# A four-layer graph network on one core: the attribute term of a perceptron is multiplied a stage earlier, and its last bias is added by GpSimd

## The chip, the cores and the metric

The kernel is written for one NeuronCore of a Trainium2 chip and is one launch. The metric is the device time of the launch in microseconds (us). The engines are TensorE (PE in the rows; its weight loads are PEld), VectorE (DVE), ScalarE (ACT), GpSimd (POOL) and SyncE (SP), which only issues transfers. All data is float32.

## The reference

12500 nodes with 128 features, 200000 edges sorted by destination. Four layers, each read from a layer norm and ReLU of `x` and added to `x`:

```
h = relu(layernorm(x)); x = x + L0(h)   # attention over edges, one head, batch norm
h = relu(layernorm(x)); x = x + L1(h)   # attention, four heads, term from edge_attr_13
h = relu(layernorm(x)); x = x + L2(h)   # perceptron, below
h = relu(layernorm(x)); x = x + L3(h)   # a table of 8 products by edge type, mean over edges

# L2
agg = segment_sum(edge_attr_128, dst)          # [12500, 128], depends on no layer
model_in = concatenate([h, agg, u[0]])         # 3 x 128
h1 = relu(model_in @ W1 + b1)
h2 = relu(h1 @ W2 + b2)
out = h2 @ W3 + b3
```

`W1` has three blocks of 128 rows: one for `h`, one for the attribute sums `agg`, one for `u` (a constant vector, folded into the first bias).

## The kernel before

Nodes lie as 128 partitions by 98 columns, handled in NK = 14 chunks of JB = 7 columns (896 values for each partition). Where a product fills PSUM banks of 512 values, a chunk is split into HALVES of 4 and 3 columns (512 and 384 values). Edges are handled in NG = 98 groups of 16 gathers.

The stages run one after another, with a barrier of all engines between them: the graph's indices, sweep A over the edges (layer L0; the 128 edge attributes are summed beside it), the nodes of L0, sweep B over the edges (layer L1, in `attention_edges`), the nodes stage `nodes_b_stage` (end of L1, all of L2, the table of L3), the sweep of L3, and the output. The nodes stage of L0 turns the attribute sums by transposes and leaves them in DRAM as `attr_turned` (features on the partitions).

**Sweep B.** GpSimd issues 16 gathers of rows of `table_b` for each group (line 1111). VectorE joins them (lines 1225 to 1290), ScalarE takes the exponentials (line 1169) and issues the stores of `sums_b` (line 1125). TensorE has nothing to do until the end of the sweep, and SyncE nothing but some loads there.

**The nodes stage.** Each engine has its own program, written by hand as a loop over i, in which work of several chunks is interleaved. In round i, among others:

- VectorE: the affine step and residual of chunk i-1 (`residual_2`, lines 1899 to 1903) with its statistics (1674 to 1681); the sum of product three and `x` for chunk i-2 (`add_product`, line 1891) and its statistics; the factors of both norms (1692, 1694); the join of chunk i (`v_join`, lines 1417 to 1433); half of the turned chunk i-1 out of PSUM (1876); `add_own` (1911) and statistics of chunk i; half of the turned chunk i-2 (1876); the factors of norm one of chunk i; the logits of chunk i+1.
- ScalarE: second ReLU of i-2 (line 1815), exponential of i (1391, with a table load), copies of three relation products (1823), roots (1685, with a table load), seven activations of norm two for i-1 (1701), a copy, seven of norm three for i-2, the other halves of the turned chunks (1810), two copies, the root of norm one, first ReLU of i-1 (1815), seven activations of norm one for i.
- TensorE: product three of i-2 (bias by a matmul with a row of ones, line 1982, then 4 and 3 products, line 1985); relation products 2 to 5 of i-3 (line 1968); turn of i-1 (1950); relation 6; turn of i-2; product one of i-1 (line 1956: `w1[:, 0, :]` with the turned `h`, `w1[:, 1, :]` with the turned attribute sums `aT`); relation 0 of i-2; product two of i-1 (1956); relation 1.
- GpSimd: only the gathers `node_sums<-sums_b` (line 1327), seven for each chunk, each chunk after the join of the chunk two before it.
- SyncE: loads of own rows, `h` and `aT` (line 1768), stores of the relation table (1773).

A matmul of float32 is shown as two instructions. Every step waits on semaphores for the steps that it reads, and nothing leaves its place in the queue of its engine.

## Time and profile before

| | us |
|---|---|
| median of three runs | 7913.9 (7896.88 to 7914.8) |
| the profiled execution | 7906.07 |
| its span, first to last instruction | 7894.7 |
| sweep B and the barrier behind it, about | 2930 to 5160 |
| the nodes stage, about | 5160 to 5563 |
| GpSimd busy over the span | 5330.8 (68%) |
| VectorE busy | 3626.2 (46%) |
| TensorE, ScalarE busy | 647.8 (8%), 534.2 (7%) |

A row of a table of stretches gives the stretch, its length, then for PE, PEld, DVE, ACT and POOL the busy time and the number of instructions, then the granted clock of TensorE as a share of 2.4 GHz, the mean busy share of the DMA engines, and GB/s. A row of a timeline gives start, duration, engine, line, operation, output<-input, shapes and count; in square brackets stands how long the engine was idle before it and what ended that. A row of the chain of waits gives start, duration and the piece of work to which the time belongs. A row of groups gives line, engine, operation, names, shapes and count, then busy time and mean ns of one, then idle time before them and what ended it.

### The profile page before, as it was taken

The numbers are of one execution on the slowest core, as the hardware profiler recorded it, in microseconds if no ns is written. First come the engines' busy times: TensorE is split into PE (matmuls) and PEld (weight loads), VectorE is DVE, ScalarE is ACT, GpSimd is POOL, SyncE is SP. The second block draws the span as 40 slices with busy tenths as digits, with TensorE's granted clock in tenths as the row PEclk, the third lists the DMA queues.
The fourth block names the chain that finished last, engine by engine and source line by source line (L and its number), as shares of the span: only waits on it lengthen the run. The fifth ranks groups of instructions, "written<-read, shape, count | busy, mean of one in ns | idle before, by whom it ended". The sixth has DMA issues, their size and how long they took to land. (4 is left out here: it accounts for less than half of the span.)

```text
span 7894.7 us, 20407 instructions
## 1 busy us (share of the span) xinstructions
PE 647.8 (8%) x2458; PEld 431.7 (5%) x2458; DVE 3626.2 (46%) x6297; ACT 534.2 (7%) x1434; POOL 5330.8 (68%) x5327
## 2 busy tenths in 40 slices
PE   1100000000000430000000000069200000000000
PEld 1100000000000430000000000034100000000000
DVE  6656666676667565344433344367222222222223
ACT  1100000000000120000000000058000000000000
POOL 5676666666664567777777777621677777777776
PEclk7555555555555665555555555579555555555555
DMA  5456666665665423333333333345333222222322
GB/s 170 127 176 188 186 194 195 195 198 185 193 196 185 143 94 116 104 104 103 98 104 104 104 104 98 99 157 212 121 97 95 94 95 95 91 94 94 95 95 89
DMA packets 324460, 1042.91 MB, mean 132 GB/s; under 512 B 101449, under 2 KB 117964, under 8 KB 286434
## 3 DMA queue, kind: packets, MB, share of 16 engines
q0 software_dynamic: 175072, 371.37, 18.5%
q1 hardware_dynamic: 92914, 452.26, 16.7%
q10 hardware_dynamic: 56336, 217.99, 7.2%
q14 instruction: 119, 0.97, 0.0%
q8 instruction: 19, 0.31, 0.0%
HBM read 527.27 MB, written 513.96 MB: 132 GB/s over the span
## 5 line engine op out<-in xcount | busy, mean ns | idle before, releaser
L2051 POOL DMA_INDIRECT edge_rows<-table_rel,rel_row x1568 | 1602.6, 1022 | 673.5 <-issue 565.3
L1111 POOL DMA_INDIRECT edge_rows<-table_b,src_i x1568 | 1640.8, 1046 | 526.7 <-issue 525.9
L1111 POOL DMA_INDIRECT edge_rows<-table_a,src_i x1568 | 1480.0, 944 | 702.9 <-issue 479.8
L2134 DVE TENSOR_TENSOR edge_rows<-edge_rows,ps 128x1024 f32<-128x1024 f32 x195 | 238.0, 1221 | 1650.6 <-DMA edge_rows<-table_rel,rel_row 1647.3
L1257 DVE TENSOR_TENSOR z<-edge_rows,dst_logit 128x16 f32<-128x16 f32 (+2 forms) x198 | 40.3, 203 | 1174.0 <-DMA edge_rows<-table_b,src_i 1141.4
L1228 DVE TENSOR_TENSOR edge_rows<-edge_rows,ps 128x1032 f32<-128x1032 f32 (+1 forms) x390 | 484.2, 1241 | 190.1 <-remote 137.3
L1225 DVE TENSOR_TENSOR ps<-edge_rows,ps 128x1032 f32<-128x1032 f32 (+1 forms) x390 | 485.7, 1245 | 53.7 <-DVE edge_rows L1228 45.7
L1290 DVE TENSOR_TENSOR edge_rows<-edge_rows,ps 128x2064 f32<-128x2064 f32 (+2 forms) x198 | 456.5, 2306 | 92.5 <-issue 68.3
L1169 ACT ACTIVATE ps<-weight_decay 128x32 f32<-128x32 f32 (+2 forms) x198 | 47.6, 240 | 4099.4 <-issue 2264.2
L844 PE MATMUL ps<-ident,edge_rows 128*128 128x128 f32 x16 | 3.9, 426 | 3902.6 <-DVE edge_rows L1210 2227.9
L1210 DVE TENSOR_TENSOR edge_rows<-edge_rows,ps 128x1024 f32<-128x1024 f32 x195 | 237.0, 1215 | 91.4 <-remote 81.0
L1202 DVE TENSOR_TENSOR ps<-edge_rows,ps 128x1024 f32<-128x1024 f32 x195 | 239.0, 1226 | 58.2 <-DVE edge_rows L1273 58.2
L2120 DVE TENSOR_TENSOR ps<-edge_rows,ps 128x1024 f32<-128x1024 f32 x195 | 239.5, 1228 | 36.0 <-DMA edge_rows<-table_rel,rel_row 29.3
L1327 POOL DMA_INDIRECT node_sums<-sums_b,sum_row x98 | 95.5, 975 | 235.6 <-DVE out_b L1433 172.7
L844 PEld LDWEIGHTS ps<-ident,edge_rows 128*128 128x128 f32 x16 | 3.1, 224 | 3903.2 <-issue 2228.2
L1968 PE MATMUL ps<-w_rel,own_part 128*128 128x512 f32 x392 | 185.6, 611 | 10.5 <-DVE rel L1883 8.9
L949 PE MATMUL ps<-ident,edge_rows 128*1 128x128 f32 (+1 forms) x16 | 3.7, 413 | 2202.9 <-DVE edge_rows L1228 2202.9
L2081 ACT ACTIVATE ps<-keep 128x16 f32<-128x16 f32 x98 | 19.6, 201 | 2111.7 <-issue 1800.4
L1273 DVE TENSOR_TENSOR edge_rows<-weight_decay,z 128x8 f32<-128x8 f32 (+1 forms) x392 | 72.1, 184 | 187.7 <-remote 121.0
L1529 POOL DMA_INDIRECT dst_logit_b<-node_logit_b,start_row x98 | 99.0, 1011 | 86.5 <-DVE node_logit_b L393 57.8
L1327 POOL DMA_INDIRECT node_sums<-sums_a,sum_row x98 | 95.9, 978 | 79.5 <-issue 31.6
L524 POOL DMA_INDIRECT dst_logit_a<-node_logit_a,start_row x98 | 101.1, 1031 | 70.6 <-ACT node_logit_a L376 39.9
(284 smaller groups left out, 2933.1 us busy)
## 6 DMA issues: line engine op xcount, KB each, us to landing
sums_a<-edge_rows SPq DMA_DIRECT2D x98, 2064.0 KB
sums_b<-edge_rows ACTq DMA_DIRECT2D x98, 1120.0 KB
edge_rows<-in_ea SPq DMA_DIRECT2D x98, 1024.0 KB
sums_rel<-edge_rows ACTq DMA_DIRECT2D x98, 1024.0 KB
table_rel<-rel SPq DMA_DIRECT2D x98, 512.0 KB
edge_rows<-table_a,src_i POOLq DMA_INDIRECT x1568
edge_rows<-table_b,src_i POOLq DMA_INDIRECT x1568
edge_rows<-table_rel,rel_row POOLq DMA_INDIRECT x1568
```

Source lines behind the costliest of these rows:

```text
L524: e.indirect_dma_start(out=A.dst_logit, out_offset=bass.IndirectOffsetOnAxis(ap=start_row[:, j:j + 1], axis=0), in_=node_a[:, j, :], in_of ...
L1111: e.indirect_dma_start(out=rows[:, s, i, 0:L.W], out_offset=None, in_=L.table, in_offset=bass.IndirectOffsetOnAxis(ap=src[:, at:at + 1], a ...
L1202: attr_step.append(then(e.tensor_tensor(old_attr, before(g, t)[:, :, L.W:L.WS], bc(keep_now[:, t, :].unsqueeze(2), [P, GK, D]), ALU.mult)))
L1210: done = e.tensor_tensor(now, now, old_attr, ALU.add)
L1225: done = then(e.tensor_tensor(heads(old), heads(before(g, t)), bc(decay_now.unsqueeze(3), [P, GK, H, C + 1]), ALU.mult))
L1228: done = e.tensor_tensor(now, now, old, ALU.add)
L1290: t_weight = then(e.tensor_tensor(now, now, bc(weights.unsqueeze(3), [P, (end - first) * GK, H, C + 1]), ALU.mult))
L1327: e.indirect_dma_start(out=self.buf[:, k % self.depth, b, :], out_offset=None, in_=self.sums, in_offset=bass.IndirectOffsetOnAxis(ap=sum_r ...
L1968: done = e.matmul(ps[:, 4 + 2 * (j % 2) + h, 0:half * D], own_part[:, j, :], w_rel[:, h * half:(h + 1) * half, :].rearrange("p r d -> p (r ...
L2051: e.indirect_dma_start(out=rows[:, s, i, :], out_offset=None, in_=table_rel, in_offset=bass.IndirectOffsetOnAxis(ap=rel_row[:, at:at + 1], ...
L2120: e.tensor_tensor(old, before, keep_now, ALU.mult).then_inc(step.sem, 1)
L2134: i = e.tensor_tensor(steps(g)[:, t, :, :], steps(g)[:, t, :, :], old, ALU.add)
```

## The change

- In sweep B, SyncE first loads the middle block of `W1`, then for each of the 14 chunks loads `attr_turned` and stores the product to a new DRAM tensor `attr_hidden`. TensorE multiplies each half of a chunk into PSUM bank 3, from the first exponential on, and ScalarE copies each half out, one in each of groups 4 to 31, ahead of its own work for the group.
- In the nodes stage `aT` holds chunks of `attr_hidden`. Product one is only the block for `h`. VectorE adds both (`add_hidden`, two instructions) into `mid1`, between the turned chunk i-2 and the factors of norm one; the first ReLU is one activation of 896 values in place.
- The third bias is added to `x` by GpSimd (`add_bias`, one instruction for a chunk) once norm two has read it. In GpSimd's queue it stands behind the gathers of the chunk two further on. The bias matmuls are gone; `add_product` waits for both.

```diff
+    attr_hidden = dram("attr_hidden", [P, NK, JB * P])
...
+            w_attr = sb("w_attr", [P, D])
+            turned = sb("attr_turned_in", [P, 2, JB * P])
+            hidden = sb("attr_hidden_out", [P, 2, JB * P])
+            w_attr_loaded = sem_of("w_attr_loaded", 16)
+            turned_loaded = [sem_of(f"attr_turned_loaded{i}", 16 * turns(NK, 2, i)) for i in range(2)]
+            attr_product = sem_of("attr_product", 2 * NK)
+            hidden_copied = sem_of("attr_hidden_copied", 2 * NK)
+            hidden_stored = [sem_of(f"attr_hidden_stored{i}", 16 * turns(NK, 2, i)) for i in range(2)]
...
+            def attr_products():
+                e.dma_start(w_attr[:, :], io["c_w1"][P:2 * P, :]).then_inc(w_attr_loaded.sem, 16)
+                for k in range(NK + 1):
+                    if inside(k):
+                        if k >= 2:
+                            e.wait_ge(*attr_product.at(2 * (k - 1)))
+                        e.dma_start(turned[:, k % 2, :], attr_turned[:, k, :]).then_inc(turned_loaded[k % 2].sem, 16)
+                    if inside(k - 1):
+                        e.wait_ge(*hidden_copied.at(2 * k))
+                        e.dma_start(attr_hidden[:, k - 1, :], hidden[:, (k - 1) % 2, :]
+                                    ).then_inc(hidden_stored[(k - 1) % 2].sem, 16)
+                for i in range(2):
+                    e.wait_ge(*hidden_stored[i].at(16 * turns(NK, 2, i)))
+
+            if L.AE:
+                attr_products()
...
+            def copy_hidden(k, h):
+                if k >= 2:
+                    e.wait_ge(*hidden_stored[k % 2].at(16 * (k // 2)))
+                i, n = HALVES[h]
+                e.wait_ge(*attr_product.at(2 * k + h + 1))
+                e.activation(hidden[:, k % 2, i * P:(i + n) * P], ps[:, 3, 0:n * P], ACT.Copy
+                             ).then_inc(hidden_copied.sem, 1)
+
...
+                if L.AE and inside(g // 2 - 2):
+                    copy_hidden(g // 2 - 2, g % 2)
...
         def tensor(e):
+            if L.AE:
+                e.wait_ge(*w_attr_loaded.at(16))
+                e.wait_ge(*exped.at(1))
+                for k in range(NK):
+                    e.wait_ge(*turned_loaded[k % 2].at(16 * (k // 2 + 1)))
+                    for h, (i, n) in enumerate(HALVES):
+                        if k + h:
+                            e.wait_ge(*hidden_copied.at(2 * k + h))
+                        e.matmul(ps[:, 3, 0:n * P], w_attr[:, :], turned[:, k % 2, i * P:(i + n) * P],
+                                 start=True, stop=True).then_inc(attr_product.sem, 1)
...
-        w1 = sb("w1", [P, 3, D])
+        w1 = sb("w1", [P, 2, D])
...
+        bias_3 = sem_of("bias_3", NK)
+        hidden_added = sem_of("attr_hidden_added", NK)
...
             def load_attr(k):
                 if k >= 2:
-                    e.wait_ge(*product_1.at(k - 1))
-                e.dma_start(aT[:, k % 2, :], attr_turned[:, k, :]).then_inc(attr_loaded[k % 2].sem, 16)
+                    e.wait_ge(*hidden_added.at(k - 1))
+                e.dma_start(aT[:, k % 2, :], attr_hidden[:, k, :]).then_inc(attr_loaded[k % 2].sem, 16)
...
         def gpsimd(e):
-            for k in range(NK):
-                nodes.p_fetch(e, k)
+            def add_bias(k):
+                if k == 0:
+                    e.wait_ge(*bars_loaded.at(48))
+                e.wait_ge(*norm2.normed.at(k + 1))
+                e.tensor_tensor(chunk(x, k), chunk(x, k), over_nodes(par[:, 2, :]), ALU.add).then_inc(bias_3.sem, 1)
+
+            for i in range(NK + 2):
+                if inside(i):
+                    nodes.p_fetch(e, i)
+                if inside(i - 2):
+                    add_bias(i - 2)
...
                 if name == "c_w1":
-                    data = data.rearrange("(a k) d -> k a d", k=P)
+                    data = data.rearrange("(a k) d -> k a d", k=P)[:, 0:3:2, :]
...
                 if inside(i - 1):
                     if i == 1:
                         e.wait_ge(*bias_1.at(1))
-                    relu(i - 1, product_1, hidden_1, mid1, 2, b12[:, 2:3])
+                    e.wait_ge(*hidden_added.at(i))
+                    e.activation(mid1[:, :], mid1[:, :], ACT.Relu, bias=b12[:, 2:3]).then_inc(hidden_1.sem, 1)
...
             def add_product(k):
                 e.wait_ge(*product_3.at(k + 1))
+                e.wait_ge(*bias_3.at(k + 1))
                 data = chunk(x, k).rearrange("p j d -> p (j d)")
...
+            def add_hidden(k):
+                e.wait_ge(*product_1.at(k + 1))
+                e.wait_ge(*attr_loaded[k % 2].at(16 * (k // 2 + 1)))
+                for h, (i, n) in enumerate(HALVES):
+                    at = slice(i * P, (i + n) * P)
+                    done = e.tensor_tensor(mid1[:, at], aT[:, k % 2, at], ps[:, 2 + h, 0:n * P], ALU.add)
+                    if h == 0:
+                        then(done)
+                done.then_inc(hidden_added.sem, 1)
...
                 if inside(i - 2):
                     turn(i - 2, h3_transposed, h3_turned_v, h3_chunk(i - 2), 0)
+                if inside(i - 1):
+                    add_hidden(i - 1)
...
-            e.matmul(ps[:, 0, 0:1], w1[:, 2, :], u0[:, :], start=True, stop=True).then_inc(u_product.sem, 1)
+            e.matmul(ps[:, 0, 0:1], w1[:, 1, :], u0[:, :], start=True, stop=True).then_inc(u_product.sem, 1)
             e.wait_ge(*bias_1.at(1))
             for i in range(NK + 3):
                 if inside(i - 2):
                     e.wait_ge(*hidden_2.at(i - 1))
-                    if i == 2:
-                        e.wait_ge(*bars_loaded.at(48))
                     for h, (a, n) in enumerate(HALVES):
-                        e.matmul(ps[:, 2 + h, 0:n * P].rearrange("p (n d) -> p n d", d=D), ones[0:1, :],
-                                 bc(par[0:1, 2, :].unsqueeze(1), [1, n, D]), start=True, stop=False)
                         for m in range(n):
                             done = e.matmul(ps[:, 2 + h, m * P:(m + 1) * P], mid2[:, (a + m) * P:(a + m + 1) * P],
-                                            w3[:, :], start=False, stop=m == n - 1)
+                                            w3[:, :], start=True, stop=True)
                     done.then_inc(product_3.sem, 1)
...
                     k = i - 1
                     for ready in (h2_turned_v, h2_turned_s):
                         e.wait_ge(*ready.at(k + 1))
-                    e.wait_ge(*attr_loaded[k % 2].at(16 * (k // 2 + 1)))
-                    product(2, [(w1[:, 0, :], hT2[:, k % 2, :]), (w1[:, 1, :], aT[:, k % 2, :])]).then_inc(product_1.sem, 1)
+                    product(2, [(w1[:, 0, :], hT2[:, k % 2, :])]).then_inc(product_1.sem, 1)
```

`over_nodes` repeats a row of 128 over the seven columns; `Signal.at(n)` is the value that a wait needs; `sem_of` shares one semaphore between stages by name.

## Rows read from the trace of the kernel before

**Rows 1.** Stretches: sweep A, sweep B, start and steady rounds of the nodes stage.

```profile
520.00:2900.00 2380.00, 162.58 (x843) 142.91 (x843) 1557.78 (x2442) 108.55 (x348) 1511.63 (x1591) 0.52 0.58 180
...
3200.00:5160.00 1960.00, 17.69 (x64) 9.37 (x64) 773.50 (x1139) 42.94 (x179) 1448.38 (x1366) 0.50 0.34 101
...
5160.00:5250.00 90.00, 42.07 (x116) 22.62 (x117) 58.54 (x221) 41.11 (x86) 36.08 (x35) 0.64 0.43 137
...
5365.00:5389.00 24.00, 22.48 (x73) 10.91 (x72) 20.27 (x76) 19.93 (x39) 6.60 (x7) 1.00 0.64 231
```

**Rows 2.** Chain of waits, one steady round of the nodes stage.

```profile
5340.74 1.02 ACT rel L1823
...
5351.25 3.01 PE ps L1956 x8
...
5359.23 1.12 PE ps L1982 x2
...
5361.44 0.84 PE ps L1982 x2
...
5364.89 1.02 ACT rel L1823
```

**Rows 3.** Timeline of the same round, VectorE and ScalarE.

```profile
5343.31 0.20 DVE L1692 RECIPROCAL norm_rs<-norm_std 128x7 f32<-128x7 f32 x1 [0.29 <-ACT norm_std L1685]
...
5346.12 1.09 DVE L1429 TENSOR_TENSOR node_sums<-node_sums,self_ex 128x896 f32<-128x896 f32 x1
...
5353.74 0.19 DVE L1692 RECIPROCAL table_rs<-table_std 128x7 f32<-128x7 f32 x1
...
5354.30 1.16 ACT L1815 ACTIVATE mid<-ps,b 128x512 f32<-128x512 f32 x2 [0.60 <-issue]
...
5355.34 2.79 ACT L1701 ACTIVATE out_b<-out_b,table_nb,table_rs 128x128 f32<-128x128 f32 x7
...
5358.17 1.09 DVE L1899 TENSOR_TENSOR out_b<-out_b,par 128x896 f32<-128x896 f32 x1 [2.71 <-ACT out_b L1701]
```

**Rows 4.** Timeline of the first rounds of the nodes stage.

```profile
5201.56 0.17 DVE L1681 TENSOR_SCALAR table_std<-table_mv 128x7 f32<-128x7 f32 x1
...
5204.32 1.16 ACT L1815 ACTIVATE mid<-ps,b 128x512 f32<-128x512 f32 x2 [2.34 <-issue]
...
5215.56 1.15 DVE L1891 TENSOR_TENSOR x<-x,ps 128x512 f32<-128x512 f32 x2 [1.73 <-PE ps L1985]
...
5231.82 1.16 ACT L1815 ACTIVATE mid<-ps,b 128x512 f32<-128x512 f32 x2 [3.51 <-issue]
```

**Rows 5.** Timeline of the last rounds of the nodes stage.

```profile
5504.80 1.09 DVE L1899 TENSOR_TENSOR out_b<-out_b,par 128x896 f32<-128x896 f32 x1 [4.03 <-ACT out_b L1701]
...
5513.71 0.20 DVE L1692 RECIPROCAL norm_rs<-norm_std 128x7 f32<-128x7 f32 x1
...
5533.47 1.15 DVE L1891 TENSOR_TENSOR x<-x,ps 128x512 f32<-128x512 f32 x2 [11.10 <-PE ps L1985]
```

**Rows 6.** Chain of waits, first rounds and last rounds.

```profile
5226.67 5.11 PE ps L1956 x8
...
5521.65 3.01 PE ps L1956 x8
...
5526.38 1.50 PE ps L1956 x4
```

**Rows 7.** Groups by shape, 5268 to 5488 us: first and second ReLU.

```profile
L1815 ACT ACTIVATE mid<-ps,b 128x512 f32<-128x512 f32 x18 | 12.2, 680 | 5.4 <-issue 4.8 <-PE ps L1956 0.6
...
L1815 ACT ACTIVATE mid<-ps,b 128x384 f32<-128x384 f32 x18 | 10.3, 571 | 0.0
```

**Rows 8.** Groups of GpSimd over the span.

```profile
L1111 POOL DMA_INDIRECT edge_rows<-table_b,src_i x1568 | 1640.8, 1046 | 526.7 <-issue 525.9 <-DMA sums_b<-edge_rows 0.8
...
L1111 POOL DMA_INDIRECT edge_rows<-table_a,src_i x1568 | 1480.0, 944 | 702.9 <-issue 479.8 <-DVE edge_rows L1228 223.1
...
L514 POOL MEMSET zero<- 128x1568 f32 x1 | 1.4, 1395 | 0.0
```

## The prediction, written before the changed kernel was run

> **What bounds the kernel now.** I read the stretches first [rows 1]. In sweep B GpSimd is busy 1448.38 of 1960 us and VectorE 773.50; TensorE (17.69) and ScalarE (42.94) are nearly idle. GpSimd's gaps are its own issue time [rows 8], so the sweep runs at its rate: (1640.8 + 526.7) / 1568 = 1.382 us for a gather. The change adds work there, but none to GpSimd or VectorE. It removes work in the nodes stage, 14 chunks in some 400 us. There, in a steady round, PE is busy 22.48 of 24 us at a granted clock of 1.00, DVE 20.27 and ACT 19.93 [rows 1]: three engines near the limit, so a share says little and the chain of waits decides.
>
> The chain [rows 2] repeats every 24.15 us (5340.74 to 5364.89). It goes ACT (relation copy, table load, roots, norms two and three), PE (turn, product one 3.01, relation, product two, relation, product three, of which the bias is 1.12 + 0.84), relation, ACT. Product one and the bias stand on it, so TensorE's side gives up 1.50 + 1.96 = 3.46 us a round. The question is what is late next, and that is read from the timeline of VectorE and ScalarE [rows 3].
>
> **The edits in sweep B.** TensorE's 28 products, ScalarE's 28 copies (0.680 or 0.571 us by the ReLUs of the same shapes [rows 7]) and 28 transfers of 448 KB go to engines and queues that wait. A copy stands ahead of the exponential of its group in ScalarE's queue, and ahead of the store of the group before; ScalarE has 98% of the sweep free, and a group takes 16 x 1.382 = 22 us. If that cover were gone, it would be 28 x 0.63 = 18 us. SyncE has nothing else to issue before the last group. The transfers share the DMA engines with the gathers: 14 x 2 x 0.46 = 13 MB. Bounds: sweep A moves 180 GB/s at a DMA share of 0.58 against 101 GB/s and 0.34, and takes (1480.0 + 479.8 + 223.1) / 1568 = 1.392 us for a gather against 1.382 [rows 1, 8]. Even if that 0.010 us were all due to the transfers, over the 512 gathers of groups 0 to 31 it makes 5 us. The other end is that each transfer holds the gathers for its own bytes: 0.46 MB at 231 GB/s [rows 1] is 2.0 us, 28 of them 56 us. I take 0; the pair of sweeps is the nearest row.
>
> **The nodes stage, steady.** I follow VectorE once around.
>
> - From the affine step (line 1899) to the factors of norm two (1692): in the round of the drain that VectorE itself sets, 5504.80 to 5513.71 is 8.91 us [rows 5]. In the steady round the same way is 5358.17 to 5343.31 + 24.15 = 5367.46, that is 9.29 [rows 3]: VectorE has only about 0.38 us of slack there.
> - From there to the point where `add_hidden` now stands, just ahead of the factors of norm one: 5343.31 to 5353.74, 10.43 us, without a wait of any length [rows 3].
> - New: two adds of 512 and 384 from PSUM, as line 1891, 1.15 us [rows 4, 5]. Product one is ready: half of it ends at 5351.25 + 1.50 = 5352.75 [rows 2], 1.0 us before.
> - New: ScalarE sees it (0.04), and the ReLU is one of 896. From 680 and 571 ns [rows 7]: 0.85 ns an element, so 680 + 384 x 0.85 = 1.01 us, and norm one starts about 0.94 after it, since the present pair of 1.16 is followed after 1.04 [rows 3].
> - From norm one on ScalarE (5355.34) to the affine step (5358.17): 2.83 us [rows 3].
>
> Sum: 8.91 + 10.43 + 1.15 + 0.04 + 0.94 + 2.83 = 24.30 us. So VectorE and ScalarE together hold the round at 24.30 where TensorE would allow some 20.7; the round gets 0.15 longer, not 3.46 shorter. The first ReLU is the hinge: now it waits for product one at 5354.30, then for VectorE, which comes to the add only at 5353.74, and ends 5355.9 instead of 5355.46. From the first steady affine step to 5504.80 there are 11 rounds: + 1.6 us.
>
> **Start and drain.** In round 1 the first ReLU waits for product one until 5204.32, VectorE is free for the add at 5201.65 [rows 4]: 5201.65 + 1.15 + 0.04 = 5202.84, 1.5 earlier, and norm one 1.6. In round 2 VectorE waits 1.73 us for product three [rows 4]; that goes: 3.3 in all. Then product one on the slow clock takes 5.11 from 5226.67 [rows 6]; with some 2.9 for its half the ReLU starts at 5226.67 - 3.3 + 2.9 + 1.19 = 5227.5 instead of 5231.82 [rows 4], and norm one is 4.4 early. At the end, product one ends 1.50 earlier, the add and wait cost 1.18, the ReLU 1.04 and a hand-over: ReLU done at 5521.65 + 1.50 + 1.18 + 1.08 = 5525.4, product two 1.0 earlier than 5526.38 [rows 6], and product three 1.96 shorter, with VectorE waiting for it [rows 5]: -2.9. Together -7.3 + 1.6 = -5.7 us.
>
> **The bias on GpSimd.** Its waits are harmless: it needs norm two of chunk k (ended 5346.6) and must be done before `add_product` of the next round, which follows product three (from 5359.23 on [rows 2]); GpSimd, queued behind it with the next gathers, waits for the join's end near 5349.3 anyway (line 1429 and two more instructions of its kind [rows 3]); a late start by 2 us of gathers that are used a round later costs nothing. But it runs while VectorE is in the join, the part of its loop in which nearly every instruction reads two operands of SBUF, and VectorE is now on the path. No row shows GpSimd reading SBUF as an operand. Its duration: a memset of 1568 elements took 1.395 us [rows 8], 0.89 ns an element, so 0.80 us for 896 with one stream and 2.4 with three (two read, one written); I take 2.0, nearer to three streams, as there are three. Its effect on VectorE: from 0 to the whole add plus one instruction under way (2.4 + 0.5 = 2.9). If it gets in before line 1431 it holds VectorE some 2.1 us, if it waits for the end of the join it holds `add_own` by some 1.5. I take 1.9 as the likelier case, a judgement. It meets a join in 13 rounds: 13 x 1.9 = + 24.7.
>
> The Trainium skill (SBUF — State Buffer, § Who interferes with whom) says that a VectorE instruction with two SBUF inputs contends with a GpSimd instruction that reads SBUF, and that whoever issues first has the shared ports for its whole instruction. No row of before can show it. By it the hold is sure; without it the sum is -5.7. The GPSIMD Engine Reference (§ 3.1, the same skill) gives 2.6 cycles an element for such an add, by which it would take an estimated 1.9 us.
>
> **Forecast.** -5.7 + 24.7 = + 19 us on the profiled execution of 7906.1, so 7925. The median of before, 7913.9, lies 7.8 higher and its runs span 18 us; I put the forecast between, at 7929.
>
> **The rivals.**
>
> 1. GpSimd and VectorE do not hold each other: -5.7, so 7908. For it: the gathers of GpSimd beside VectorE's joins leave line 1429 at 1.09 us. Against it: those gathers read little. Chance 0.27.
> 2. The add holds VectorE for longer, in 13 rounds over 2.3 us: 13 x 2.9 - 5.7 = + 32, 7946. It is slower by more than 0.3% from 2.3 us a round. Chance 0.14.
> 3. The transfers slow the gathers in sweep B. Half of the upper end, 28 us, on top of the forecast: 7957. Against it sweep A's rate. Chance 0.07.
> 4. TensorE's clock falls in the steady rounds, as PE will be busy 19 of 24 to 26 us. It is granted 1.00 at 22.48 of 24 and 0.64 as the mean of the start, where PE is busy 42.07 of 90 [rows 1]. At 1.2 GHz PE's 19 us would be 38, and a round 14 us longer; if it happens in four of them, + 56 us, 7985. Chance 0.05.
> 5. The round follows TensorE and ScalarE after all, because VectorE runs its loop faster than my walk: ScalarE's 19.93 busy plus its two short waits make 22.8, so 11 x -1.35 - 7.3 = -22, 7892. Against it: the walk's terms are VectorE's own. Chance 0.05.
>
> The forecast has 0.42. A measurement of this kernel can tell some 0.3% (24 us) from no change. Slower: the upper part of the forecast (0.07), rivals 2, 3 and 4 nearly whole (0.23): 0.30. Faster: half of rival 5 and a little of rival 1 with the spread of the runs (0.03): 0.06. Within: 0.64. The range takes in rival 1 with half the spread of the runs and rival 2 with some of it: 7898 to 7955.
>
> **What would show it.** Right: the steady round is about 26.2 us; the first ReLU ends the idle time of ScalarE after VectorE's add, not after a product; VectorE waits for norm one less than 2.71 us, PE waits more; one instruction of the join in each round starts or lasts some 2 us late beside GpSimd's add; the sweep's 98 groups take what they took, within 5 us. No hold: round of 24.3 us and all join instructions at 1.09. Wrong altogether: a steady round below 23.5 us, PE's clock below 1.00 in steady rounds, gathers above 1.40 us each, or VectorE waiting for product one.

## The result and the profile after

The changed kernel takes 7919.45 us (median of 17 runs, 7910.24 to 7938.63); the kernel before, on the same chip, 7909.85 (17 runs, 7891.21 to 7920.99). The ratio is 1.0015 with a 95% interval of 1.0009 to 1.0022: slower by 0.15%, 9.6 us. The forecast was 7929, within 7898 to 7955. The profiled execution took 7917.39 with a span of 7906.2, so 11.3 us more than that of before (7906.1, 7894.7).

The page of the changed kernel, groups of GpSimd, beside [rows 8]:

```profile
L1120 POOL DMA_INDIRECT edge_rows<-table_b,src_i x1568 | 1636.6, 1044 | 530.9 <-issue 530.9
...
L1120 POOL DMA_INDIRECT edge_rows<-table_a,src_i x1568 | 1480.9, 944 | 708.1 <-issue 478.1
...
L1845 POOL TENSOR_TENSOR x<-x,par 128x896 f32<-128x896 f32 x14 | 33.8, 2417 | 195.4 <-ACT hn L1746 195.4
```

A gather of sweep B still takes (1636.6 + 530.9) / 1568 = 1.382 us, to the third digit what it took before. The new add takes 2417 ns in the mean.

The stretches answering to [rows 1] (sweep B, the start of the nodes stage, a part of a steady round, and two whole steady rounds; columns: the stretch, its length, busy us of PE, PEld, DVE, ACT and POOL with instructions, granted clock, DMA share, GB/s):

```profile
3200.00:5158.00 1958.00, 48.86 (x100) 18.16 (x100) 773.14 (x1138) 51.08 (x198) 1443.86 (x1366) 0.50 0.36 105
5158.00:5248.00 90.00, 37.15 (x110) 19.99 (x110) 67.47 (x227) 43.99 (x91) 42.33 (x39) 0.63 0.44 142
5367.00:5391.00 24.00, 18.05 (x60) 8.43 (x58) 21.11 (x65) 19.14 (x38) 9.08 (x8) 1.00 0.60 213
...
5341.00:5367.00 26.00, 20.48 (x66) 9.67 (x65) 23.03 (x79) 20.19 (x39) 9.09 (x8) 1.00 0.62 222
5393.00:5419.00 26.00, 20.54 (x64) 9.95 (x63) 23.04 (x77) 20.28 (x38) 9.08 (x8) 0.93 0.56 203
```

In sweep B TensorE has 31 us more work and ScalarE 8, and GpSimd's and VectorE's sums stay. In the nodes stage VectorE is now the busiest engine, 23.03 of 26 us. The chain of waits over one round says the same (start, length, what it was in), beside [rows 2], where VectorE hardly stood:

```profile
5335.24 1.10 DVE out_b L1967
...
5344.15 0.21 DVE norm_rs L1737
...
5347.02 1.03 DVE node_sums L1474
5348.05 2.91 DVE own_rows L1476
5350.98 1.09 DVE out_b L1478
...
5356.48 1.15 DVE mid L1959 x2
5357.65 1.04 ACT mid L1920
5358.69 1.95 ACT out_b L1746 x6
...
5361.42 1.10 DVE out_b L1967
```

The affine step (line 1899 before, 1967 now) comes every 26.18 us, and up to the ReLU at 5357.65 the chain never leaves VectorE. One of three neighbours in the join, all of the same shape, takes 2.91 us where the others take 1.03 and 1.09. The timeline shows who is beside it:

```profile
5346.95 1.09 DVE L1474 TENSOR_TENSOR node_sums<-node_sums,self_ex 128x896 f32<-128x896 f32 x1
5347.53 2.46 POOL L1845 TENSOR_TENSOR x<-x,par 128x896 f32<-128x896 f32 x1 [12.91 <-ACT hn L1746]
5347.96 2.98 DVE L1476 TENSOR_TENSOR own_rows<-own_rows,self_ex 128x896 f32<-128x896 f32 x1
```

GpSimd's add runs 5347.53 to 5349.99. VectorE's L1476 is issued at 5347.96 and ends at 5350.94, 0.95 after the add: it did nearly all of its work of 1.08 only once the add was over, and lost 1.90.

Where the time went, on the two profiled executions:

| stretch | before | after | difference |
|---|---|---|---|
| up to the first load of the nodes stage | 5160.27 | 5158.03 | -2.2 |
| from there to the third affine step | 75.42 | 72.47 | -2.95 |
| 11 rounds to the last affine step | 269.11 | 288.20 | +19.1 |
| drain, to the first load of the next stage | 57.84 | 55.44 | -2.4 |
| the rest | 2332.07 | 2332.01 | -0.1 |

The 11 rounds would have cost 11 x (26.18 - 24.15) = 22.3; the 3.2 that are missing were two long rounds of before, in which a relation product ran at the lower clock (chain of the kernel before; the granted clock is 1.00 over the first of these pieces and 0.57 over the second):

```profile
5307.48 1.72 PE ps L1968 x4
...
5313.43 3.12 PE ps L1968 x4
```

In 5393 to 5419 of the changed kernel the granted clock is 0.93 as well, and the round still takes 26.18: TensorE has slack now. Of the -2.2 ahead of the stage, 1.8 lie behind the last gather of sweep B, where both kernels do the same: from its end to the first load of the stage it is 58.8 us before and 57.0 after. It is scatter: two kernels below that share the changed sweep, with the memset and with the short add, take 57.0 and 58.8 there too.

### The profile page after: what moved, and what is told of

It is laid out like the page before. It is cut to its first block and busy times, and to the rows that moved or that the text cites. A ratio compares the mean times of both kernels' runs of the same rounds, so it can differ in the third digit from the quotient of the medians.

```text
span 7906.2 us, 20448 instructions
## 1 busy us (share of the span) xinstructions
PE 657.9 (8%) x2402; PEld 425.0 (5%) x2402; DVE 3663.6 (46%) x6325; ACT 548.0 (7%) x1448; POOL 5355.3 (68%) x5341
## 5 line engine op out<-in xcount | busy, mean ns | idle before, releaser
L1120 POOL DMA_INDIRECT edge_rows<-table_b,src_i x1568 | 1636.6, 1044 | 530.9 <-issue 530.9
L1845 POOL TENSOR_TENSOR x<-x,par 128x896 f32<-128x896 f32 x14 | 33.8, 2417 | 195.4 <-ACT hn L1746 195.4
```

Of the source, the lines that this page charges most:

```text
L1120: e.indirect_dma_start(out=rows[:, s, i, 0:L.W], out_offset=None, in_=L.table, in_offset=bass.IndirectOffsetOnAxis(ap=src[:, at:at + 1], a ...
```

## The experiments

All were timed or profiled beside the kernel before on the same chip. Chips differ: on two, no gather was slowed (944 ns in both sweeps) and the kernel before takes 7100 us instead of 7910. The steady rounds of the nodes stage are the same on all of them, so I compare these ("round" is the usual distance of two affine steps), and beside them the stage's length from its first load to that of the next stage. The length scatters more: for the nodes stage of before it is 402.4 us in the trace of [rows 1 to 6] and 399.4 in that of the sweep-only kernel below.

### The bias left out

```diff
             for i in range(NK + 2):
                 if inside(i):
                     nodes.p_fetch(e, i)
-                if inside(i - 2):
-                    add_bias(i - 2)
...
-                e.wait_ge(*bias_3.at(k + 1))
```

> The third bias is left out of the computation: GpSimd's adds and VectorE's waits for them are gone, all else is as after the change. Theory: in each of 13 rounds GpSimd's add holds one instruction of VectorE's join (2.98 us instead of 1.09) through the SBUF access they share, and VectorE's own loop sets the round. Then the steady round is 24.3 us (26.18 with the add), the second instruction of the join lasts 1.09, and the time is some 24 us below the changed kernel and 5 to 12 us below the kernel before. Rival one: the round grew because of VectorE's added instructions and the longer way to the first ReLU, and the held instruction only fills a wait: the round stays above 25.5 us. Rival two: TensorE sets the round once the add is away: below 23.5 us and more than 20 us below the kernel before.

Measured: 7094.11 us against 7100.51, ratio 0.999 (0.9981 to 0.9999). Stage 393.4 us, round 24.28 us (timeline, VectorE):

```profile
4751.57 1.09 DVE L1964 TENSOR_TENSOR out_b<-out_b,par 128x896 f32<-128x896 f32 x1 [2.22 <-ACT out_b L1746]
...
4764.28 1.08 DVE L1476 TENSOR_TENSOR own_rows<-own_rows,self_ex 128x896 f32<-128x896 f32 x1
4765.40 1.09 DVE L1478 TENSOR_TENSOR out_b<-own_rows,node_sums 128x896 f32<-128x896 f32 x1
...
4775.85 1.09 DVE L1964 TENSOR_TENSOR out_b<-out_b,par 128x896 f32<-128x896 f32 x1 [2.21 <-ACT out_b L1746]
```

L1476 is back at 1.08. The walk of the prediction gave 24.30 for a round without a hold; here it is, 24.28. From there to 26.18 are 1.90 us, and by 1.90 one instruction of each round is longer in the changed kernel.

### The bias part alone, and the attribute part alone

The first has the third bias on GpSimd as the changed kernel, and layer one as before. The second has the sweep's products and VectorE's `add_hidden`, and the bias on TensorE:

```diff
                     for h, (a, n) in enumerate(HALVES):
+                        e.matmul(ps[:, 2 + h, 0:n * P].rearrange("p (n d) -> p n d", d=D), ones[0:1, :],
+                                 bc(par[0:1, 2, :].unsqueeze(1), [1, n, D]), start=True, stop=False)
                         for m in range(n):
                             done = e.matmul(ps[:, 2 + h, m * P:(m + 1) * P], mid2[:, (a + m) * P:(a + m + 1) * P],
-                                            w3[:, :], start=True, stop=True)
+                                            w3[:, :], start=False, stop=m == n - 1)
```

> The kernel before with only the bias edit: the bias matmuls go, GpSimd adds the bias after norm two, product one keeps both blocks. Theory: the hold is there without the attribute edit, the second or third instruction of the join lasts 2.9 us in 13 rounds. VectorE has no add of the hidden part, so its loop is 1.15 us shorter: way to norm one 10.43 + 1.83 + 0.40, then 2.83 and 8.91, a round of 24.4 us; against the kernel before (24.16 in its undisturbed rounds, 24.46 on average) no difference in the steady rounds and 2 to 4 us less at start and drain. Rival (the hold needs the added instructions of the attribute edit, or does not matter): join instructions of 1.09 and a round of 23.8.

> The changed kernel with only the attribute edit: the bias is a matmul again, GpSimd adds nothing. Theory: VectorE sets the round at 24.3 us although TensorE has its 1.96 us of bias back, no join instruction above 1.1 us; the time is some 2 us above the kernel without any bias (start and drain), 3 to 10 us below the kernel before. Rival (TensorE is still on the path): the round is longer than without the bias by up to 1.96 us.

Measured: bias alone 7100.51 us, ratio 1.0 (0.9991 to 1.001), round 24.73, stage 399.6. Attribute part alone 7109.45 us, ratio 1.0014 (1.0005 to 1.0023), stage 409.0, with six rounds of 24.67 and five of 26.3.

Bias alone, timeline of a round:

```profile
4762.74 1.09 DVE L1910 TENSOR_TENSOR out_b<-out_b,par 128x896 f32<-128x896 f32 x1 [1.76 <-ACT out_b L1701]
...
4775.03 2.46 POOL L1799 TENSOR_TENSOR x<-x,par 128x896 f32<-128x896 f32 x1 [11.47 <-ACT hn L1701]
4775.46 2.98 DVE L1431 TENSOR_TENSOR own_rows<-own_rows,self_ex 128x896 f32<-128x896 f32 x1
...
4787.47 1.09 DVE L1910 TENSOR_TENSOR out_b<-out_b,par 128x896 f32<-128x896 f32 x1 [1.76 <-ACT out_b L1701]
```

The hold is there in full, 2.98 against 1.08, yet the round is only 0.57 above the 24.16 of before. It is also 0.3 above the 24.4 that I expected, and the 2 to 4 us of gain did not come: the time is that of the kernel before.

Attribute part alone, timeline of a long round and a piece of a usual one:

```profile
4732.79 1.09 DVE L1964 TENSOR_TENSOR out_b<-out_b,par 128x896 f32<-128x896 f32 x1 [2.21 <-ACT out_b L1746]
...
4737.95 2.77 PE L2035 MATMUL ps<-w_rel,own_part 128*128 128x512 f32 x3
4741.20 1.02 ACT L1877 ACTIVATE rel<-ps 128x1024 f32<-128x1024 f32 x1 [4.01 <-PE ps L2035]
4743.78 0.20 DVE L1737 RECIPROCAL norm_rs<-norm_std 128x7 f32<-128x7 f32 x1 [1.99 <-ACT norm_std L1730]
...
4759.15 1.09 DVE L1964 TENSOR_TENSOR out_b<-out_b,par 128x896 f32<-128x896 f32 x1 [2.21 <-ACT out_b L1746]
...
4765.87 1.02 ACT L1877 ACTIVATE rel<-ps 128x1024 f32<-128x1024 f32 x1 [2.33 <-PE ps L2035]
...
4783.82 1.09 DVE L1964 TENSOR_TENSOR out_b<-out_b,par 128x896 f32<-128x896 f32 x1 [2.21 <-ACT out_b L1746]
```

I had expected this one below the kernel before, and it came 9 us above it. Between affine step and the factors of norm two, ScalarE waits 2.33 us for the relation product that stands behind product three and its bias, and the factors come 9.30 us after the affine step instead of 8.91. In the long rounds, where the granted clock of 4734 to 4758 is 0.93 and three of its matmuls take 2.77 together, it waits 4.01. From the kernel without any bias this one differs by the bias matmuls alone, so they keep TensorE on the path: 24.67 against 24.28, and rounds that the lower clock can lengthen. So my theory for this kernel was wrong and its rival right. The attribute part needs TensorE relieved of the bias; the bias part, on VectorE, is dearer beside the attribute part (next experiment).

### The add moved behind VectorE's join

```diff
             def add_bias(k):
                 ...
                 e.wait_ge(*norm2.normed.at(k + 1))
+                if inside(k + 1):
+                    e.wait_ge(*added_h1.at(k + 2))
                 e.tensor_tensor(chunk(x, k), chunk(x, k), over_nodes(par[:, 2, :]), ALU.add).then_inc(bias_3.sem, 1)
```

Once on the changed kernel, and once on the kernel with the bias part alone (here twice, in two sessions).

> The changed kernel, all of the computation, with one more wait in GpSimd's bias add: it waits until VectorE has done the add of h1 for the next chunk. There VectorE has some 4 us in which no instruction reads two operands from SBUF (statistics, a copy from PSUM, the add from PSUM). Theory of the shared read access: GpSimd's add of 2.4 us runs beside them without holding anything, the join's instructions last 1.09, the round is 24.3 us, the time 20 us or more below the changed kernel and 5 to 12 us below the kernel before. GpSimd's gathers start 3.7 us later in a round, which costs nothing. Rival (any VectorE instruction beside GpSimd's add is held): the statistics or the copies take the 1.9 us instead and the round stays at 26 us.

> The kernel before with the third bias on GpSimd, its add held back until VectorE's own-row add of the next chunk is issued; the attribute part stays on TensorE. Theory (the hold is all that the bias part costs, 1.9 us in a round of 24.73 us in which TensorE also had less to do): no join instruction over 1.2 us, steady round 23.8 us, between 22.8 and 24.1, and 4 to 10 us under the kernel before. Rival (the round is set by something that the hold only hides behind): round stays at 24.7 us.

> The kernel with the third bias on GpSimd behind VectorE's own-row add and nothing else of the change, once more and in another session, because where the gathers of sweep B are slowed (1.38 us each and not 1.25) the rest of the kernel is 800 us longer. Theory (the gain lies in the nodes stage alone): that stage within 1 us of 389.3 and 10 to 16 us under the kernel before, whatever the gathers do. Rival (the gain came with the session): within 5 us of the kernel before.

The changed kernel with the add moved: 7093.19 us against 7100.51, ratio 0.999 (0.9981 to 0.9999); round 24.28, stage 393.2, as without any bias.

```profile
4766.52 1.09 DVE L1478 TENSOR_TENSOR out_b<-own_rows,node_sums 128x896 f32<-128x896 f32 x1
...
4768.13 1.08 DVE L1981 TENSOR_TENSOR out_b<-out_b,h 128x896 f32<-128x896 f32 x1
...
4769.36 2.09 POOL L1847 TENSOR_TENSOR x<-x,par 128x896 f32<-128x896 f32 x1 [13.52 <-DVE out_b L1981]
4770.73 0.58 DVE L1723 BATCH_NORM_AGGREGATE table_mv<-stats 128x2 f32<-128x6 f32 x7
```

The add now lies beside VectorE's statistics, which read one operand; nothing is held (every join instruction 1.08 or 1.09), and the add itself is shorter, 2.09 instead of 2.46. So the add costs nothing by its own length: all of its price was the place. 7.3 us under the kernel before is within the 5 to 12 expected.

The bias part alone with the add moved: 7087.09 us against 7099.18, ratio 0.9984 (0.9975 to 0.9993), the fastest kernel here; round 23.77 (theory 23.8), stage 389.3. The gain of 12.1 us is larger than the 4 to 10 expected.

```profile
4804.36 1.09 DVE L1912 TENSOR_TENSOR out_b<-out_b,par 128x896 f32<-128x896 f32 x1 [2.73 <-ACT out_b L1701]
...
4821.03 2.09 POOL L1801 TENSOR_TENSOR x<-x,par 128x896 f32<-128x896 f32 x1 [12.28 <-DVE out_b L1924]
...
4824.25 1.16 ACT L1827 ACTIVATE mid<-ps,b 128x512 f32<-128x512 f32 x2 [0.59 <-PE ps L1969]
...
4828.12 1.09 DVE L1912 TENSOR_TENSOR out_b<-out_b,par 128x896 f32<-128x896 f32 x1 [2.74 <-ACT out_b L1701]
```

Here the first ReLU waits 0.59 us for TensorE's product one, so VectorE has slack just behind the join; that is why the same hold cost this kernel only 24.73 - 23.77 = 0.96. The rest of its 1.90 came out of VectorE's wait for norm one ahead of the affine step, 2.74 here and 1.76 with the hold. In the changed kernel `add_hidden` puts VectorE itself in front of that ReLU, and the hold costs all of its 1.90. In the other session: 7899.55 against 7908.21, ratio 0.999 (0.998 to 0.9999), stage 386.8 against the 402.4 in the trace of [rows 1 to 6]. The stage was 2.5 shorter than I expected and the time 8.7 lower, between the rival's 5 and my 10 to 16; medians of runs that span 34 us don't settle that, the stage does: it is 12.6 below even the 399.4 of the sweep-only kernel, so the gain is there.

### The changed kernel again, the sweep's part alone, and a copy given to ScalarE

The sweep-only kernel has all of the diff ahead of the nodes stage, and the nodes stage of before. The third is the changed kernel with the add moved and

```diff
-        by_vector = (3,)
+        by_vector = ()
...
                     relation(i - 3, 2)
+                    relation(i - 3, 3)
                 if inside(i - 1):
                     norm2.s_root
```

> The changed kernel itself, unaltered, for a comparison with its variants on one chip. Theory (the bias add holds one VectorE instruction in each round): steady round 26.2 us, one join instruction of 2.9 to 3.0 us in each round against 1.09 for its neighbours, time 8 to 16 us above the kernel before. Rival (the loss was a matter of the chip on which it was first timed): within 3 us of the kernel before.

> Only the second sweep's part of the change: the products with the attribute rows of the first layer's weights, their copies and stores; the nodes stage is that of the kernel before, and what is stored is not read. Theory (the sweep is held by the gathers): sweep B within 1 us of before per 98 groups, time within 5 us of the kernel before. Rival (its loads, products and copies slow the sweep): 10 to 50 us slower.

> The changed kernel with the bias add held back until VectorE's own-row add of the next chunk is issued, and the fourth relation copy of each chunk (1.22 us on VectorE) done by ScalarE behind the third. Theory (the round is now the chain of VectorE and ScalarE, and VectorE's copy is on it): root of norm two 0.3 us later, VectorE's 1.22 us gone, so a round of 23.4 us against 24.28 with the add moved alone, about 10 us less over the stage; TensorE no longer waits 2.4 us for that copy. Rival (ScalarE becomes the bound): round 24.6 us or more, slower than with the add moved alone.

The changed kernel: 7116.18 us against 7099.18, ratio 1.0025 (1.0015 to 1.0035); round 26.18, 13 held instructions of 2.86 to 2.98, stage 416.1. The loss is no matter of one chip; at +17.0 it is nearer to the forecast's +19 here, and 1 us above the 8 to 16 that I expected of this run.

The sweep's part: 7099.49 against 7099.18, ratio 1.0001 (0.9992 to 1.001), gathers at 1.25 us, as in the kernel with the bias part alone on the same chip, whose sweep is that of before. It is free within the interval of 0.1%.

The copy on ScalarE: 7095.39 us, ratio 0.9995 (0.9986 to 1.0004), rounds of 24.3 to 25.0, 24.6 in the mean, not 23.4.

```profile
4787.49 1.02 ACT L1881 ACTIVATE rel<-ps 128x1024 f32<-128x1024 f32 x1 [0.69 <-PE ps L2039]
4788.53 1.28 ACT L1730 ACT_TABLE_LOAD   x1
...
4790.06 0.20 DVE L1737 RECIPROCAL norm_rs<-norm_std 128x7 f32<-128x7 f32 x1 [0.84 <-ACT norm_std L1730]
...
4800.17 1.15 DVE L1962 TENSOR_TENSOR mid<-aT,ps 128x512 f32<-128x512 f32 x2 [0.40 <-PE ps L2027]
...
4805.13 1.09 DVE L1970 TENSOR_TENSOR out_b<-out_b,par 128x896 f32<-128x896 f32 x1 [2.21 <-ACT out_b L1746]
```

ScalarE can't start the fourth copy before its product is there (0.69 of waiting), and the table load and the roots stand behind it: the factors of norm two come 9.84 us after the affine step instead of 8.92. That eats 0.92 of the 1.22 us that VectorE saves. The rest doesn't reach the round either: from the factors on, the chain of waits runs over ScalarE's norms and TensorE's product one, and VectorE's new add, which had been the last to come, now waits for that product (0.40). The theory took ScalarE's waits for room; the rival, ScalarE as the bound, was right.

### What GpSimd does while VectorE is held

The add's place in the changed kernel, with another instruction in it: a memset, a multiplication by 1.0 from one source, and the add on 3 of 7 strands. None of the three adds the whole bias, so they tell of time alone. Each was executed once, beside one execution of the kernel before (7925.54, 7934.16 and 7922.01 us against 7929.8); one execution is too little for a time of the launch, so I read their rounds.

```diff
-                e.tensor_tensor(chunk(x, k), chunk(x, k), over_nodes(par[:, 2, :]), ALU.add).then_inc(bias_3.sem, 1)
+                e.memset(scratch[:, 0, :, :], 0.0).then_inc(bias_3.sem, 1)
```
```diff
+                e.tensor_scalar(scratch[:, 0, :, :], chunk(x, k), 1.0, None, ALU.mult).then_inc(bias_3.sem, 1)
```
```diff
+                e.tensor_tensor(chunk(x, k)[:, 0:3, :], chunk(x, k)[:, 0:3, :], over_nodes(par[:, 2, :])[:, 0:3, :],
+                                ALU.add).then_inc(bias_3.sem, 1)
```

> The changed kernel with GpSimd's bias add replaced by a memset of a buffer of its own of the same 128x896 elements (the third bias is left out of the result). Theory (GpSimd's reading is what shuts VectorE out): the join instruction behind it stays at 1.09 us, steady round 24.3 us. Rival (any GpSimd instruction on SBUF holds VectorE while it lasts, about 1.4 us by the memset of the kernel before): the instruction takes 1.8 to 2.1 us, round 25.0 to 25.3.

> The changed kernel with GpSimd's bias add replaced by a multiplication of the same 128x896 elements by 1.0 into a buffer of its own: one source instead of two (the third bias is left out of the result). Theory (one source read is enough for the hold): one join instruction of 2.3 to 2.9 us in each round, steady round 25.4 to 26.2 us. Rival (the hold needs two sources on GpSimd too): every join instruction at 1.09 us, round 24.3 us.

> The changed kernel with the bias added by GpSimd to 3 of the 7 strands of a chunk, 128x384 elements instead of 128x896 (the rest of the third bias is left out of the result). Theory (VectorE is held until the add has ended): the add takes 2.09 x 3/7 = 0.9 us plus what it waits itself, so 0.9 to 1.3; it starts 0.43 us before the join instruction that it holds, which then takes 1.6 to 2.0 us; round 24.8 to 25.2. Rival (a fixed price for each meeting of the two engines, whatever the add's length): still 2.98 us and a round of 26.2.

A steady round of each, in this order (timelines of three kernels):

```profile
5346.90 0.84 POOL L1846 MEMSET scratch<- 128x896 f32 x1 [12.91 <-ACT hn L1746]
5347.36 1.08 DVE L1476 TENSOR_TENSOR own_rows<-own_rows,self_ex 128x896 f32<-128x896 f32 x1
```
```profile
5348.15 2.82 POOL L1846 TENSOR_SCALAR scratch<-x 128x896 f32<-128x896 f32 x1 [12.89 <-ACT hn L1746]
5348.58 1.82 DVE L1476 TENSOR_TENSOR own_rows<-own_rows,self_ex 128x896 f32<-128x896 f32 x1
...
5350.43 1.09 DVE L1478 TENSOR_TENSOR out_b<-own_rows,node_sums 128x896 f32<-128x896 f32 x1
```
```profile
5360.97 1.37 POOL L1845 TENSOR_TENSOR x<-x,par 128x384 f32<-128x384 f32 x1 [12.93 <-ACT hn L1746]
5361.40 1.89 DVE L1476 TENSOR_TENSOR own_rows<-own_rows,self_ex 128x896 f32<-128x896 f32 x1
```

| GpSimd beside the join | its length | VectorE's L1476 | round | stage |
|---|---|---|---|---|
| nothing | | 1.08 | 24.28 | 393.4 |
| memset, 896 | 0.84 | 1.08 | 24.30 | 392.7 |
| one source, 896 | 2.82 | 1.82 | 25.03 | 399.5 |
| add, 384 | 1.37 | 1.89 | 25.10 | 400.6 |
| add, 896 | 2.46 | 2.98 | 26.18 | 416.1 |

Writing alone holds nothing: not GpSimd's presence but its reading shuts VectorE out. The memset was shorter than the 1.4 us by which I had priced the rival, and ends 0.4 us after L1476 has begun, so in a steady round that rival would show as 0.25 us only (an end 0.95 after the memset's). The first of the 13 rounds tells more, because there the memset starts just ahead of the join's last instruction:

```profile
5227.04 0.85 POOL L1846 MEMSET scratch<- 128x896 f32 x1 [6.12 <-ACT hn L1746]
...
5227.17 1.09 DVE L1478 TENSOR_TENSOR out_b<-own_rows,node_sums 128x896 f32<-128x896 f32 x1
```

By the rival this instruction would have taken 1.67; it took 1.09. In the same place the changed kernel has the add, and 2.92. In both adds VectorE ends 0.95 after the add (5363.29 against 5362.34; 5350.94 against 5349.99), so the hold follows the add's length and is no fixed price. The rivals of the memset and of the short add are out (the short add itself took 1.37, above my 0.9 to 1.3; its hold and its round came as expected). With one source VectorE ends 0.57 *before* GpSimd (5350.40 against 5350.97): it is held 0.74 and lasts 1.82, far less than my 2.3 to 2.9. The next one, L1478, has two operands as well, starts 0.54 before the multiplication ends, and takes its plain 1.09. That the hold lasts for GpSimd's whole instruction is thus shown for the add only; why the one-source form lets go earlier, these runs don't tell. (The stage with the full add is 22.7 longer than the 393.4 without one; 11 x 1.90 makes 20.9 of that, and most of the other 1.8 are two more holds, in the first rounds.)

## Why the prediction was right, step by step

- **Sweep B costs nothing.** Right: 1.382 us for a gather before and after, and the sweep's part alone made 0.3 us on 7099. Neither the transfers (DMA share 0.34 to 0.36) nor the copies reached GpSimd's path.
- **The walk round VectorE.** Each term has its row in the chain of after: affine step to the factors of norm two 5335.24 to 5344.15 = 8.91 (predicted 8.91); from there to the new add 5356.48 - 5344.15 = 12.33 (10.43 + 1.90 of hold); the add and the hand-over 1.17 (1.19); ReLU and norm one to the affine step 3.77 (0.94 + 2.83). Sum 26.18, predicted about 26.2; without the hold 24.28, predicted 24.30. That TensorE's 3.46 us a round buy nothing is what the experiment without the bias shows: PE is busy only 19.8 of 24.28 there, and the round is no shorter than the 24.16 of before.
- **The add's length.** Taken at 2.0 us, it was 2.46. Two reasons. Alone it is 2.09 for 896 elements and 0.99 for 384 (the last add of a run, which has no join beside it): 2.15 ns an element and 0.17 us for the instruction. And the add, too, is held: VectorE's L1474 is under way when it starts, which makes 2.09 into 2.46. The other adds of the changed kernel bear this out: where the instruction under way has 0.07 us left the add takes 2.08, with 0.5 left 2.44 to 2.46, with 0.69 left 2.64. The estimate by the Trainium skill (GPSIMD Engine Reference, § 3.1), 2.6 cycles an element, 1.9 us, agrees in its slope; it has neither the 0.17 nor the wait.
- **The hold.** Taken at 1.9 "a judgement", measured 1.90 in 11 steady rounds. The value is partly luck: it came out of an add taken too short and a meeting point taken too vaguely. An add meets a join in 13 rounds, as predicted; the two in the first rounds fall on the last instruction of the join, and cost 1.6 us together (from the first load to the third affine step 72.31 with the add, 70.74 without), not 3.8. The Trainium skill (SBUF — State Buffer, § Who interferes with whom) states this rule nearly as the rows have it: a two-source VectorE instruction against a GpSimd instruction that reads SBUF, the later one waiting, and no conflict with one that only writes or with a VectorE instruction of one source. Its words "for the whole instruction" stand there at VectorE's two-port modes; the prediction took them over to two-operand instructions. The memset and the moved add agree, with 0.0 us of hold. The one-source multiplication, which held 0.74 of its 2.82, does not fit "for the whole instruction", while the adds do.
- **Start, drain and the sum without a hold.** -5.7 was predicted if nothing is held; the kernel without the bias is 6.4 us under the kernel before, the one with the add moved 7.3. Of the start and the drain, -4.4 and -2.9 predicted: without the hold the start is 74.13 - 70.74 = 3.4 shorter, the drain 56.19 - 55.61 = 0.6 in those two runs; on the first chip, the drain of before was 57.84 and the gain 2.4. So the start is right within 1 us; the drain of one and the same stage differs by 1.6 between those two traces of it, and how much of 2.9 is real stays open.
- **The sum.** +19 on the profiled execution, measured +11.3 there, and +17.0 between the medians on the second chip. The 7.7 between 19 and 11.3 are: two long rounds of before that I took as 24.15 each (3.4), the start, where I gave the two holds too much (2.3), the scatter ahead of the stage (2.2), less 0.5 of drain, and 0.2 between the span and the execution's own time (11.5 against 11.3).
- **The rivals.** The round after TensorE and ScalarE: no, it is 26.18, and 24.28 without the hold. No hold: refuted by 13 instructions of 2.86 to 2.98. A longer hold: no. Transfers against gathers: no. TensorE's clock: it is 0.93 over single rounds, but there was slack for it. (The price was also too high: it doubled PE's time, where product one in [rows 2, 6] takes 5.11 against 3.01.) The clock turns up where I hadn't placed it, in the attribute part alone.

## What to carry to other kernels

Before an elementwise operation goes to GpSimd, look at what VectorE does in the very microseconds in which it would run: beside instructions with two SBUF operands the add of 2.46 us cost 1.90 on the critical engine, beside a statistics pass nothing, and a memset beside the join cost nothing, and one more semaphore wait may be enough to choose. A part that relieves one engine is worth only what the next one leaves; try the parts of a change one by one, since here the half with the bias moved (-12 us) is better than the whole with the bias moved (-7 us), and much better than the whole as given (+17 us on such chips; each against the kernel before on its own chip).

## What the runs showed of the hardware

- Gathers of the same code take 944 ns each in both sweeps on two chips and 1.04 us in sweep B on the others, with the gaps between them longer too (1.25 against 1.38 us a gather). The changed kernel's span is 787 us longer on the first chip (7906.2 against 7119.1): 208 of that are sweep B and 342 lie ahead of it; behind it 20 come up to the nodes stage and 218 after it, and the nodes stage itself takes 416.1 on both. What sets it is open.

```profile
L1120 POOL DMA_INDIRECT edge_rows<-table_b,src_i x1568 | 1481.7, 945 | 477.8 <-issue 477.8
```

- GpSimd's memset of 896 elements takes 0.84 us, the multiplication of one source by a constant 2.45 without a join beside it, longer than the add of two sources (2.09).
- VectorE's hold shows as a longer instruction, not as idle time: no view of waits lists it. One looks for unlike durations of a like shape.
